# A decoder on one core: each engine's queue of the merged stage in an order of its own, and half of cross attention's exponentials from scores that GpSimd has lowered

## The reference, cut to what matters

```python
_layernorm(v) = (v - mean) / sqrt(var + 1e-5)
# 1 encoder: 4 layers of linear attention and feed forward (128 -> 512 -> 128)
    h = _layernorm(x, ln1_s, ln1_b)
    qp, kp = elu(h @ Wq + bq) + 1.0, elu(h @ Wk + bk) + 1.0
    kv, ksum = einsum('bshd,bshm->bhmd', kp, v), sum(kp, axis=1)
    x = x + (einsum(qp, kv) / (einsum(qp, ksum) + 1e-6)) @ Wo + bo
    x = x + relu(_layernorm(x, ln2_s, ln2_b) @ W1 + b1) @ W2 + b2
# 2 cross attention over ctx, 16 heads of 8 features, the mask hides keys
    scores = where(mask == 0, -1e9, einsum('bhqd,bhkd->bhqk', q, k) / sqrt(8))
    x = x + (softmax(scores) @ v) @ Wo.T + bo
# 3 feed forward with a convolution and quantized operands
# 4 attention over the 64 nearest keys of each query, 16 heads
    _, idx = lax.top_k(scores, 64); logits = where(in_top_64, scores, -inf)
    x = x + (softmax(logits) @ v) @ w_out_w.T + b
# 5 channel attention   6 eight experts, silu(x @ wg) * (x @ wu) @ wd, summed
```

## Time and profile before

| | |
|---|---|
| median of 3 runs | 1575.99 us (1571.63 to 1576.9) |
| the profiled execution's own time | 1575.56 us |
| its span in the trace | 1572.7 us, so 2.9 us lie around it |
| mean granted TensorE clock | 0.785 |
| busy in the span | PE 1100.0 us (70%), DVE 1009.3 (64%), ACT 694.9 (44%), POOL 449.9 (29%) |
| exponentials of cross attention half 0 begin | 222.0 us |
| first turn with `nmax` to the last | 436.0 to 766.5 us |
| last exponential of cross attention half 1 | 902.3 us |

### The profile page before, as it was taken

How to read it: one execution, slowest core, us unless ns; L and a number is a source line. 1 busy time by engine, 2 the same in 40 slices (tenths; PEclk the granted TensorE clock), 3 DMA queues, 4 the chain that set the end, 5 groups by cost and what they waited for, 6 DMA issues and landing times. The chain is left out here.

```text
span 1572.7 us, 17058 instructions
## 1 busy us (share of the span) xinstructions
PE 1100.0 (70%) x4698; PEld 646.6 (41%) x4698; DVE 1009.3 (64%) x3062; ACT 694.9 (44%) x1983; POOL 449.9 (29%) x422
## 2 busy tenths in 40 slices
PE   3887836554657278777675655477999758898788
PEld 2676613322444245445442323233444324454333
DVE  6665686687477787777737678467666786644322
ACT  2443448542555145554117833564666335332121
POOL 4322335104344044433123402443222232201000
PEclk9998957657676687676655766598999868899899
DMA  3101100000000000000010000011111101111121
GB/s 115 27 27 27 27 27 1 1 0 0 1 27 2 12 16 1 19 9 1 1 48 1 1 0 0 8 41 41 41 54 41 40 21 41 54 61 41 49 78 47
DMA packets 34125, 41.22 MB, mean 26 GB/s; under 512 B 5280, under 2 KB 19248, under 8 KB 34032
## 3 DMA queue, kind: packets, MB, share of 16 engines
q1 hardware_dynamic: 33360, 38.21, 7.9%
q0 software_dynamic: 672, 1.98, 0.4%
HBM read 39.13 MB, written 1.05 MB: 26 GB/s over the span
## 5 line engine op out<-in xcount | busy, mean ns | idle before, releaser
L1877 DVE TENSOR_TENSOR big<-psum,qe 128x512 f32<-128x512 f32 x128 | 87.8, 687 | 218.4 <-PE psum L1401 102.9
L977 ACT ACTIVATE qe<-psum 128x512 f32<-128x512 f32 x128 | 75.1, 596 | 203.1 <-PE psum L1392 203.0
L1382 PE MATMUL psum<-big,wexp 128*128 128x512 f32 x256 | 137.8, 623 | 0.0
L872 ACT ACTIVATE far<-far,half_far,fmul 128x128 bf16<-128x128 bf16 x256 | 103.0, 482 | 52.4 <-DVE hit L1655 52.4
L828 ACT ACTIVATE Wk<-S,nsm 128x128 f32<-128x128 f32 x256 | 98.7, 387 | 16.0 <-DVE nsm L2108 16.0
L1668 DVE MAX8 near<-Wk 128x8 f32<-128x128 f32 x512 | 103.5, 275 | 0.3
L1201 PE MATMUL psum<-ctxT,kT 32*128 32x512 f32 x128 | 52.9, 909 | 70.2 <-DVEq L1744 43.4
L567 POOL TENSOR_SCALAR veps<-mv 128x4 f32<-128x4 f32 x34 | 8.2, 241 | 306.5 <-DVE mv L1577 306.5
L1401 PE MATMUL psum<-hT,wexp 128*128 128x512 f32 x128 | 71.1, 639 | 20.8 <-DVE big L1877 20.8
L1073 PE MATMUL psum<-ident,h 128*128 128x128 f32 x176 | 37.1, 340 | 68.6 <-DVE h L1584 52.9
L1584 DVE TENSOR_SCALAR h<-xs,mv,rstd 128x128 f32<-128x128 f32 x128 | 55.6, 496 | 43.7 <-POOL rstd L569 40.5
(11 more groups left out here) (312 smaller groups left out, 2731.4 us busy)
## 6 DMA issues: line engine op xcount, KB each, us to landing
wexp<-in_mg SPq DMA_DIRECT2D x32, 256.0 KB, 2.7
wexp<-in_mu SPq DMA_DIRECT2D x32, 256.0 KB, 3.0
wexp<-in_md SPq DMA_DIRECT2D x32, 256.0 KB, 3.5
w<-in_aw SPq DMA_DIRECT2D x8, 256.0 KB, 2.9
w<-in_w2a SPq DMA_DIRECT2D x8, 256.0 KB, 2.6
ctxt<-in_ctx SPq DMA_DIRECT2D x8, 256.0 KB, 4.1
wqkv<-in_aw SPq DMA_DIRECT2D x8, 192.0 KB, 2.3
xin<-in_x SPq DMA_DIRECT2D x4, 256.0 KB, 3.2
```

Source lines behind the costliest of these rows:

```text
L872: ins = act.activation(far[t][:, hd, :], far[t][:, hd, :], ACT.Identity, bias=half_far[:, 0:1], scale=fmul[t][:, hd:hd + 1])
L977: act.activation(sg[k % 2], bank(5 + k % 2), ACT.Silu).then_inc(silu_done, 1)
L1382: pe.matmul(bank(4), wd[e % 2][:, c, :], hid[k % CH], start=(k % NCHUNK == 0), stop=(k % NCHUNK == NCHUNK - 1), skip_group_check=True).the ...
L1877: dve.tensor_tensor(hid[k % CH], bank(U_BANK[k]), sg[k % 2], ALU.mult).then_inc(hu_done, 1)
```

## The change

**The merged stage.** Each engine gets a function `merged_turn(b)` with the parts of a turn in an order of its own, and the common points go. The parts keep their instructions, with two exceptions: the relu of the keys (128x512) moves from GpSimd to ScalarE, and GpSimd's subtraction of the penalties (128x2048) becomes two of 8 heads each.

The parts of the diff follow. What all engines share (banks of the cross prologue, buffers of the turned context):

```diff
+CROSS_BANKS = (((2, 3, 0, 1), (6, 7, 4, 5)), ((3, 4, 5, 5), (6, 7, 4, 5)))
...
+        ctxT_of = [[t[:, :] for t in ctxT], [flat(t) for t in at]]
```

GpSimd (`tensor_tensor`, here and below, is `out, in0, in1, operation`):

```diff
+                def less_maximum(b):
+                    pool.wait_ge(m_done, hf * NB + b + 1)
+                    pool.tensor_tensor(S[b % 3][:, 8:H, :], S[b % 3][:, 8:H, :], smax[b % 2][:, 8:H].unsqueeze(2).to_broadcast([P, 8, P]), ALU.subtract).then_inc(x_less, 1)
+                less_maximum(0)
                 for b in range(1, NB):
                     a = b - 1
+                    less_maximum(b)
                     pool.wait_ge(z_done, hf * NB + (a + 1))
                     pool.tensor_tensor(E[a % 2][:, :, :], E[a % 2][:, :, :], zden[a % 2][:, :].unsqueeze(2).to_broadcast([P, H, P]), ALU.mult).then_inc(x_prob, 1)
                     if b + 2 < NB:
...
+            def less_penalties(b, part):
+                t = b % 2
+                heads = slice(8 * part, 8 * part + 8)
+                pool.wait_ge(z_ready, 3 * b + 1)
+                pool.wait_ge(far_done, 2 * b + part + 1)
+                pool.tensor_tensor(Wk[t][:, heads, :], Wk[t][:, heads, :], far[t][:, heads, :], ALU.subtract).then_inc(z_ready, 1)
...
+            def merged_turn(b):
+                if 0 <= b < NB:
+                    signed_scores(b)
+                if 0 <= b < STEPS:
+                    feed_base(b)
+                if 1 <= b + 2 < NB:
+                    spread_keys(b + 2)
+                if 0 <= b < NB:
+                    less_penalties(b, 0)
+                    less_penalties(b, 1)
+                if 0 <= b - 1 < NB:
+                    spread_queries(b - 1)
+                if 0 <= b + 1 < STEPS:
+                    attend_base(b + 1)
+                if 0 <= b < STEPS:
+                    step_rsqrt("A", b + 2)
+                if 0 <= b + 1 < STEPS:
+                    step_rsqrt("F", b + 1)
+                if 0 <= b < NB:
+                    maxima_in_parts(b)
```

ScalarE:

```diff
-                for hd in range(H):
-                    ins = act.activation(E[a % 2][:, hd, :], S[a % 3][:, hd, :], ACT.Exp, bias=nsm[a % 2][:, hd:hd + 1],
-                                         scale=RSQRT_DH, accum_out=zden[a % 2][:, hd:hd + 1])
-                ins.then_inc(exp_done, 1)
+                for hd in range(8):
+                    act.activation(E[a % 2][:, hd, :], S[a % 3][:, hd, :], ACT.Exp, bias=nsm[a % 2][:, hd:hd + 1],
+                                   scale=RSQRT_DH, accum_out=zden[a % 2][:, hd:hd + 1])
+                act.wait_ge(x_less, hf * NB + (a + 1))
+                act.activation(E[a % 2][:, 8:H, :], S[a % 3][:, 8:H, :], ACT.Exp, scale=RSQRT_DH).then_inc(exp_done, 1)
...
+                    act.activation(kp[s], kk[s][:, :, :], ACT.Relu).then_inc(k_relu, 2)
...
+            def merged_turn(b):
+                here, old, new = 0 <= b < NB, 0 <= b - 2 < NB, 0 <= b + 1 < NB
+                step, fed = 0 <= b + 1 < STEPS, 0 <= b < STEPS
+                if 0 <= b - 1 < NB:
+                    maxima(b - 1)
+                if step:
+                    attend(b + 1, "input")
+                if here:
+                    penalties(b, range(0, 6))
+                if old:
+                    exponentials(b - 2, 0)
+                if step:
+                    attend(b + 1, "queries")
+                if fed:
+                    feed(b, "input")
+                if step:
+                    attend(b + 1, "keys")
+                if here:
+                    penalties(b, range(6, 11))
+                if old:
+                    exponentials(b - 2, 1)
+                if fed:
+                    feed(b, 0)
+                if here:
+                    penalties(b, range(11, H))
+                if fed:
+                    feed(b, 1)
+                if new:
+                    scores_out(b + 1, 0)
+                    scores_out(b + 1, 1)
+                    signs(b + 1, range(0, 4))
+                if step:
+                    attend(b + 1, "attended")
+                if new:
+                    signs(b + 1, range(4, H))
+                if b == 5:
+                    attended_out(0, 6)
```

TensorE:

```diff
+            def merged_turn(b):
+                before, old, new = 0 <= b - 1 < NB, 0 <= b - 2 < NB, 0 <= b + 1 < NB
+                step, fed = 0 <= b + 1 < STEPS, 0 <= b < STEPS
+                if step:
+                    attend(b + 1, "input")
+                if before:
+                    turned_maxima(b - 1)
+                if old:
+                    turned_scores(b - 2, 0)
+                if step:
+                    attend(b + 1, "projections")
+                if fed:
+                    feed(b, "input")
+                if old:
+                    turned_scores(b - 2, 1)
+                if b == 6:
+                    pe.wait_ge(n_x, NX_AT["project", 0])
+                if fed:
+                    feed(b, 0)
+                if old:
+                    outputs(b - 2, 0)
+                    outputs(b - 2, 1)
+                if step:
+                    attend(b + 1, "sums")
+                if fed:
+                    feed(b, 1)
+                if old:
+                    outputs(b - 2, 2)
+                    outputs(b - 2, 3)
+                if new:
+                    scores(b + 1, 0)
+                if step:
+                    attend(b + 1, "attention")
+                if fed:
+                    feed(b, "down")
+                if new:
+                    scores(b + 1, 1)
+                if step:
+                    attend(b + 1, "attended")
+                    attend(b + 1, "output")
+                if before:
+                    settled_rows(b - 1)
...
+                for b in range(-1, NB + 2):
+                    merged_turn(b)
+                    if b == 5:
+                        attended_turned(0, 6)
+                        pe.wait_ge(x_upd, 2 * norm_no("A", b + 2)[1])
+                        attended_projected(0, 7)
+                    if b == NB:
+                        pe.wait_ge(x_upd, 2 * norm_no("A", STEPS + 1)[1])
+                        context_turned(1)
+                    if b == NB + 1:
+                        for s in SL:
+                            cross_queries(s, 1)
+                        pe.wait_ge(pk_done, nth(1, 3))
+                        attended_turned(1, 6)
+                        pe.wait_ge(pv_done, nth(1, 3))
+                        attended_projected(1, 7)
```

VectorE:

```diff
+                dve.tensor_reduce(zden[a % 2][:, 8:H], E[a % 2][:, 8:H, :], AX.X, ALU.add).then_inc(x_max, 1)
+                dve.wait_ge(x_max, 2 * (hf * NB + a) + (2 if a == NB - 1 else 3))
...
+            def merged_turn(b):
+                here, before, old = 0 <= b < NB, 0 <= b - 1 < NB, 0 <= b - 2 < NB
+                step, fed = 0 <= b + 1 < STEPS, 0 <= b < STEPS
+                if b == 6:
+                    attended_added(0, 7)
+                if here:
+                    sides(b)
+                if before:
+                    nearest(b - 1, range(0, H), 0)
+                if step:
+                    attend(b + 1, "projections")
+                if before:
+                    replaced(b - 1, range(0, 8))
+                if step:
+                    attend(b + 1, "queries")
+                    attend(b + 1, "keys")
+                if before:
+                    replaced(b - 1, range(8, H))
+                    nearest(b - 1, range(0, 4), 8)
+                if step:
+                    attend(b + 1, "sums")
+                if before:
+                    nearest(b - 1, range(4, H), 8)
+                if step:
+                    attend(b + 1, "attention")
+                if before:
+                    thresholds(b - 1)
+                if fed:
+                    feed(b)
+                if before:
+                    mark_dropped(b - 1)
+                if step:
+                    attend(b + 1, "output")
+                if old:
+                    head_outputs(b - 2)
+                if fed:
+                    step_normalize("A", b + 2)
+                if before:
+                    unsettled_rows(b - 1)
+                if here:
+                    maxima(b)
+                if step:
+                    step_normalize("F", b + 1)
+                if before:
+                    settle(b - 1)
             def beside_encoder():
-                for t in range(-PTS, (NB + 2) * PTS):
...
+                for b in range(-1, NB + 2):
+                    if b == NB + 1:
+                        for s in SL:
+                            normalize(s, NLN + LN_B)
+                        for s in SL:
+                            cross_values(1, s)
+                    merged_turn(b)
+                    if b == NB:
+                        for s in SL:
+                            encoded(1, s)
+                            dve.wait_ge(x_upd, both(s, NUP + LN_B))
+                            layer_norm(s, NLN + LN_B)
                 attended_added(1, 7)
...
```

(8 more changed lines are left out.)

292 lines of the change are left out of this document (130 added, 162 removed).

## The result

The changed kernel takes 1503.74 us (median of 4 runs, 1503.53 to 1509.17) against 1576.45 (median of 4); the ratio is 0.9544 with a 95% interval of 0.9501 to 0.9586. That is 72 us less, where 26 less was forecast: right in sign, and outside the range, whose low end was 1522.

What follows compares the result with a forecast made beforehand. TensorE's queue, work plus waits, was taken as the path of regular turns, ScalarE as nearest the bound in cross attention. -14 - 4.8 + 1 - 2 - 1 - 1 - 3 = -24.8 from 1575.6 gave 1550.8, said as 1550; range 1522 to 1570.

Steps and rivals of the forecast that it cites:

- the regular turns: Merged stage: a turn goes from 45.95 to 43.2 us, -2.8 each, -14 over five turns.
- the waits shrink and the clock rises: Rival, chance 0.20: at clock 0.80 a regular turn is 38.3 us, total about 1523 to 1527.
- a clock of 0.68 in turns just as full: Argument against the rival of a rising clock: the granted clock was 0.68 in turns just as full.
- the signs of being wrong: Turns under 40 at clock 0.8, `at` wait staying, long search moved over 2 us, last-`nmax`-to-cross-attention stretch over 5.
- The waits removed: Regular turns, TensorE: attended rows 3.4, settled count 2.2, exponentials 2.0 and hidden chunk 1.5 go, together 9.1 us.
- The head: Start of a regular turn: `nmax` behind the encoder's update leaves some 7.0 us of wait against 2.0, +5.0.
- Blocking: VectorE held up beside GpSimd's 128x2048 operations, 5.2 us a turn; shortening it counted at nothing (bounds 0 and -5.2).
- First turn: First window, 43.0 us: VectorE's idle before its normalization (4.37) and a little blocking go, -4.8.
- Last turn: Last window, 38.9 us: waits of 2.2, 2.0 and 1.5 go, head gains 5.0; -2 (-5 to +3).
- Cross attention: Pair of 18.6 us loses some 0.9, seven pairs -6, stage ends add 1.2 to 1.5: -3 (-8 to +6).
- Prologue: End of stage and prologue, 46.9 us: context part moves ahead of turn 9, -1 (-5 to +3).
- Half 1's top-64 attention: Top-64 attention of half 1: the halved subtraction hides as before, 0 (-1 to +1).

Runs made afterwards that it cites:

- the dummy work: Unused dummy transposes ahead of TensorE's waits at a turn's end, added to the kernel before: 1562.78 us, ratio 0.9944.
- the changed kernel's second profile: The changed kernel, nothing altered, run once more for comparison on the same chip: 1502.94 us, ratio 0.9565.
- the merged turns' alone: The changed kernel with cross attention put back as it was before the change: 1511.55 us, ratio 0.9617.

## Why the prediction was wrong

**The step that failed** is in the regular turns: "a turn becomes 34.2 + 7.0 + 0.7 + 1.3 = 43.2". The three waits in it were measured at 7.2 and 2.5 against 7.0 and 2.0, and the idle time at 8.65 against 9.0. The 34.2 was taken over from before as a constant, and was 30.2, because TensorE's level is high for more of its work (0.807 instead of 0.717, weighted by busy time). This is 4.0 of the 4.4 us by which each turn was missed; the five turns are 20 of the 46 us in all. The rival "the waits shrink and the clock rises" had it, with 38.3 for a turn against 38.8 measured, and 0.20 of the chance; the dummy work (1562.78 in the old order, with the kernel's own work at 29.2 to 29.8 us a turn) shows that the clock is the mechanism. That its 38.3 came so near was in part luck: it took a mean clock of 0.80 over time where 0.76 was measured, and 1.5 us of the head as hidden where no more than 0.35 was. What spoke against it in the prediction, a clock of 0.68 in turns just as full, was no evidence: those turns had the same scattered waits. Of the signs of being wrong that the prediction gave, two came: turns under 40 us, and a stretch behind the last `nmax` that changed by more than 5 (6.9).

**The waits removed**: right. All four entries went; putting one back (3.4 forecast) cost 3.4 a turn.

**The head**: right in size (7.2 in the turn shown and 6.2 in the mean, against 7.0), and confirmed by taking the maxima's part away.

**Blocking**: in the turns it vanished (5.0 us a turn) though the prediction left it standing, and by the order more than by the halves: with the whole subtraction in the new order VectorE is busy 30.1 us a turn, not 34.5. One reading in the prediction was off: the normalization of 3.53 us starts at 646.35, behind the end of the 128x2048 operation (641.27 and 3.61 long), beside three short GpSimd operations. Costing it at nothing in a turn came out: TensorE's idle time was missed by 0.35 us only, and the old order with the blocking whole had the same gain in busy time. No run puts the blocking back into the new order, so up to those 0.35 us remain possible.

**First turn**: mis-sized, -7.8 against -4.8. **Last turn**: -2 forecast, +0.6 in the profile shown, but 31.2 to 31.6 us in eight other profiles with merged turns, the changed kernel's second one (31.4) among them, which is -7.5. So it was mis-sized too, and the profile shown hides that by chance. The two lie side by side here, first the changed kernel's and then the merged turns' alone, TensorE only:

```profile
679.00:709.00 30.00, 25.01 (x90) 0.50 0.00 1
709.00:718.50 9.50, 2.59 (x19) 0.68 0.00 1
```

```profile
686.90:701.00 14.10, 9.14 (x35) 0.50 0.01 1
701.00:718.10 17.10, 10.27 (x73) 0.90 0.00 1
```

Same orders, same wait of 8.3 us (4.6 of them inside the stretch), 107 and 108 groups; in one the level rises after some 14 us and in the other after some 30, and the latter costs 8.2 us more. Such differences probably make the spread of 10 to 20 us between the runs of one kernel (the kernel before: 1562.8 us at a mean clock of 0.791, 1583.1 at 0.779).

**Cross attention**: the mechanism was right, two terms were mis-sized. A pair takes 17.3 us against the 17.8 worked out (the subtraction 1.90 against 1.8, the exponential of 128x1024 1.04 against 1.1); from the first masked copy to the last that is -4.7 and -3.9 in the two halves rather than -3 each. And each stage's end was given +1.2 to +1.5 where it is 1.8 and 2.1 shorter (last masked copy to last exponential 11.3 before, 9.5 and 9.2 after), since the last sequence's exponentials are two us shorter too. The chain is the one that was forecast: ScalarE idles 4.4 us of the pair shown, and TensorE's longest wait in it is the one ahead of the transposes, for GpSimd's multiplication:

```profile
PE psum L1214 <- POOL Wk L615: 6.2, 2, 4.5
```

By the Trainium skill's rule in "GPSIMD Engine Reference", "Engine selection", the subtraction was to be nearer 2.3 than 1.8; the trace has 1.90, nearer to the row.

**Prologue**: the bounds were -5 to +3, taken -1, measured -6.9; putting it back, in a looser order, cost 12. **Half 1's top-64 attention**: "0, hides as before" failed; 6.4 us of the 9.8 lie in the interval behind the ninth `nmax`, and they come with the halved subtraction. What was costed at nothing there is the wait of VectorE's normalization beside it (2.44 us instead of 4.37), and the level of TensorE behind it (0.92 instead of 0.83). The other 3.4 weren't traced; in the changed kernel's second profile they are 0.8.

**Left open**: what sets how long the level stays low once TensorE works again (after the wait of 8.3 us it rose after 9.14 us of work in one execution, and after 25.01 of nearly unbroken work in another), and why it fell for 3.1 us in the midst of unbroken work (624.8 above). The Trainium skill, "TensorE: Matmul & The Clock Gate", Part 1, says that idleness brings the low level and activity releases it; the dummy work agrees, the 25.01 us of work at 0.50 above don't fit it.

## What to carry to other kernels

When an edit moves waits about on TensorE, don't carry its busy time over from the profile before: weight the granted clock by busy time, stretch by stretch, and price a turn at both levels. A wait joined to one that is already long cost its length here; waits of the same sum scattered through the work also cost the clock behind them (0.717 against 0.808). Where an order can't be mended further, dummy transposes in a wait can buy the level back, 0.6 to 2.9 us in some 40 here. And look for short operations of VectorE that start just behind a long one of GpSimd: halving the long one freed 2 us of VectorE here.

## What the hardware showed that was not expected

- TensorE stayed at the low level for 25.01 us of work after a wait of 8.3 us, and for 9.14 where the same instructions ran in another kernel.
- With 12.0 us of idle time a turn in few places TensorE's clock, weighted by busy time, was 0.808; with 11.8 us in many, 0.717.
- Dummy transposes made both kernels faster by about 12 us (1562.78 against 1574.70 in the old order, ratio 0.9944; 1490.76 against 1503.74 in the new).
- Halving one GpSimd subtraction of 4.07 us, with nothing else changed, was worth 0.8% (0.9918, 0.989 to 0.9946) in the old order and nothing measurable in the total of the new (0.9565 against 0.9588).
